# Decoder block: order of the first layer's scan decays on ScalarE, one half step moved ahead of the rotary block, one Newton step fewer

## The reference

```
x = x + attention0(layernorm(x))            # 8 heads, 2 kv heads, d = 32, rotary, window 64, softcap 30
x = x + ssm0(ctx, gate = layernorm(x))      # scan over ctx (4, 256, 128), 256 channels, 16 states
x = x + ffn0(layernorm(x))                  # 704 wide, SiLU gate
```

```
u     = silu(conv(in_proj(ctx)) + b)                    # 256 channels
dt, B, C = x_proj(u)                                    # 8 + 16 + 16 rows
delta = softplus(dt_proj(dt) + b)
state = state * exp(delta * A) + (delta * u) * B_t      # per channel and per state n of 16
y     = sum_n(state_n * C_n) + D * u ;  y *= silu(gate)
```

## Time and profile before

| | |
|---|---|
| median of 3 runs | 913.36 us (910.98 to 916.4) |
| the profiled execution's own time | 913.75 us |
| its span, first to last instruction | 912.0 us |
| mean granted TensorE clock | 0.924 |
| busy: PE / DVE / ACT / POOL | 767.7 / 703.3 / 445.6 / 340.6 us |
| chain that ended last | PE 50%, DVE 26%, issue 11%, ACT 9% |

### The profile page before, as it was taken

The page is one execution under the profiler, slowest core; times in us unless marked ns, Lnnn a source line. Parts: engine busy times, 40 slices in busy tenths (PEclk is TensorE's granted clock), DMA queues, the critical chain, the costliest instruction groups (busy, mean ns, idle before and its releaser), DMA issues.

```text
span 912.0 us, 12288 instructions
## 1 busy us (share of the span) xinstructions
PE 767.7 (84%) x3984; PEld 563.1 (62%) x3984; DVE 703.3 (77%) x1229; ACT 445.6 (49%) x928; POOL 340.6 (37%) x242
## 2 busy tenths in 40 slices
PE   6771459877798996799999999999955799999997
PEld 2241346554433563477767776777743689999996
DVE  4869779889857976999999999999977544444443
ACT  1663368650336402666566556756642354444442
POOL 1001346552330422233333323432343286666663
PEclk9785579998799998999999999999987899999999
DMA  4313223345020212011111211111300243334431
GB/s 171 121 47 114 93 94 125 115 139 218 1 98 0 74 43 92 19 40 44 51 36 36 69 36 36 55 39 36 118 0 1 79 158 138 138 138 138 141 135 46
DMA packets 28884, 74.63 MB, mean 82 GB/s; under 512 B 3633, under 2 KB 6337, under 8 KB 28449
## 3 DMA queue, kind: packets, MB, share of 16 engines
q1 hardware_dynamic: 28384, 71.51, 23.2%
q10 hardware_dynamic: 448, 2.49, 0.8%
HBM read 72.55 MB, written 1.44 MB: 81 GB/s over the span
## 4 chain that ended last, share of the span: by engine, by line
PE 50%; DVE 26%; issue 11%; ACT 9%; POOL 3%; DMA 1%; POOLq 0%; DVEq 0%; SPq 0%; ACTq 0%
PE ps L1671 6%; PE ps L1785 6%; PE ps L1786 6%; PE ps L1787 6%; PE ps L1631 4%; DVE hS L976 3%; PE ps L1651 3%; PE ps L1750 3%; PE ps L1435 2%; PE ps L1738 2%; DVE arena L1280 2%; DVE hS L1006 2%; DVE ps L968 2%; PE ps L1408 1%; PE ps L1720 1%
## 5 line engine op out<-in xcount | busy, mean ns | idle before, releaser
L403 POOL TENSOR_TENSOR hS<-hS,BCb 128x512 f32<-128x512 f32 x64 | 81.6, 1278 | 131.9 <-issue 66.7
L1387 DVE SCALAR_TENSOR_TENSOR arena<-ps,arena 128x1024 f32<-128x1024 f32 x32 | 39.2, 1224 | 102.2 <-ACT arena L842 93.1
L426 POOL TENSOR_TENSOR hS<-hS,BCb 128x1024 f32<-128x1024 f32 x23 | 56.1, 2440 | 111.3 <-DVE ps L968 96.3
L1671 PE MATMUL ps<-WB,hT 128*128 128x512 f32 x192 | 88.0, 603 | 3.0 <-DVE arena L1261 2.0
L476 POOL TENSOR_TENSOR MHl<-arena,MHh 128x1024 fp32r<-128x1024 f32 x34 | 81.7, 2404 | 16.9 <-ACT MHh L845 16.9
L1416 PE MATMUL ps<-ident,hS 128*128 128x128 f32 x256 | 40.1, 311 | 54.7 <-POOL hS L426 31.2
L1785 PE MATMUL ps<-Wh,MHh 128*128 128x256 f32 x272 | 77.8, 286 | 6.0 <-POOL MHl L476 6.0
L1006 DVE TENSOR_TENSOR_SCAN hS<-dA,ps 128x512 f32<-128x512 f32 x64 | 78.1, 1220 | 2.2
L1786 PE MATMUL ps<-Wl,MHh 128*128 128x256 f32 x272 | 77.6, 285 | 0.0
L1787 PE MATMUL ps<-Wh,MHl 128*128 128x256 f32 x272 | 77.5, 285 | 0.0
L1416 PEld LDWEIGHTS ps<-ident,hS 128*128 128x128 f32 x256 | 32.6, 159 | 65.1 <-POOL hS L426 38.2
(11 more groups left out here) (233 smaller groups left out, 1967.4 us busy)
## 6 DMA issues: line engine op xcount, KB each, us to landing
BCb<-bc_dram SPq DMA_DIRECT2D x32, 512.0 KB, 3.7
BCb<-bcq_dram SPq DMA_DIRECT2D x64, 256.0 KB, 3.1
arena<-gate_dram SPq DMA_DIRECT2D x32, 512.0 KB, 3.7
WB<-in_we SPq DMA_DIRECT2D x34, 256.0 KB, 2.7
WB<-in_wqkv SPq DMA_DIRECT2D x1, 3072.0 KB, 12.7
WA<-in_wo ACTq DMA_DIRECT2D x1, 2048.0 KB, 7.7
WA<-in_ffn SPq DMA_DIRECT2D x1, 1408.0 KB, 7.9
pkb<-in_pk SPq DMA_DIRECT2D x2, 698.0 KB, 4.7
```

Of the source, the lines that this page charges most:

```text
L403: gp.tensor_tensor(h, h, qbc(q)[:, 1:2, :].broadcast_to([P, DT, S]), ALU.mult).then_inc(s["c_ready"], 1)
L426: gp.tensor_tensor(h, h, BCb[g % SB_LOADS][:, 1:2, :].broadcast_to([P, DT, HALF]), ALU.mult).then_inc(s["c_ready"], 1)
L1671: last = mm(ps[:, bank + t, :], hT[:, c, P * (2 * b + t):P * (2 * b + t) + P], WB[:, c, c0:c0 + 512], start=(c == 0), stop=(c == HC - 1))
```

## The change

On ScalarE the decays of half steps 1, 2 and 3 are issued in a row, ahead of `xdbl_copy(1)`. Before, those of half step 1 stood between the copy and the softplus, those of 2 behind the softplus, those of 3 behind the eight projection copies. On VectorE half step 3 is run ahead of the rotary block and not behind it. The reciprocal square root has three Newton steps and not four.

```diff
             steps_to(0)
             d_u(0)
+            steps_to(3)
             xdbl_copy(1)
-            steps_to(1)
             softplus(1)
             softplus_ln(1)
-            steps_to(2)
             for t in range(NT):
                 act.wait_ge(s["qkv0_mm"], t + 1)
                 sc.copy(Q0[:, t, :], ps[:, 4 + t % 4, 0:NQKV0]).then_inc(s["qkv0_copied"], 1)
-            steps_to(3)
             d_u(1)
...
             delta_u(1)
+            ssm_step(3)
             dve.wait_ge(s["qkv0_copied"], NT)
...
-            for g in range(3, 6):
+            for g in range(4, 6):
                 ssm_step(g)
...
-            for k in range(4):
+            for k in range(3):
...
-                if k < 3:
+                if k < 2:
```

## The result

The change makes the kernel faster, by less than forecast: 911.38 us median (908.92 to 914.04) against 913.59 (910.98 to 923.67), 20 runs each; ratio 0.9968 with a 95% interval of 0.9955 to 0.9981. The ratio makes 2.9 us (1.7 to 4.1), where 4.89 were forecast; the two medians lie 2.2 us apart. The profiled execution took 910.91 us, its span is 909.1, the mean granted clock 0.923.

A forecast was written before the change was run, and what follows sets the result against it. Order of work bounds the early part, VectorE's own work the later. 4.01 us gained at half step 4's scan (8.46 idle removed, 4.36 added) and 0.88 from the Newton step make 4.89: median 908.5 us, range 904.5 to 914.

The forecast's parts named there:

- Decays ahead, VectorE up to the block: Before the rotary block: early decays fit ScalarE's idle time at no cost; VectorE is free for the block 3.64 us sooner.
- The eight copies: Projection copies ahead of the rotary block: TensorE goes on without a stop, the last ends at 57.7, before VectorE's 58.80.
- The added wait: Ahead of half step 4's scan: VectorE waits 4.36 us for decays queued behind the square of the heads and a table load.
- Newton step: In the reciprocal square root ahead of L1111: three dependent instructions go, and the whole 0.88 us is gained.
- L1111: VectorE's scaling of the heads, ahead of the first attention: starts at 92.66 instead of 97.55, 4.89 us earlier.
- To the end: From L1111 to the kernel's end: the 4.89 us lead arrives whole, as nothing there is tied to a point in time.
- rival of a cheaper start: At the attention's 32 transposes: TensorE's clock rises earlier against them; about 1.5 us more gives 907.0; chance 0.10, faster.
- The range and the sign: For the whole kernel: a gain, with the time between 904.5 and 914 us.
- the chance of faster by over 0.5%: For the whole kernel: faster 0.56, against within 0.5% 0.36 and slower 0.08.
- The rivals on the clock: Projection copies late, about 911, chance 0.10; transposes cheaper, 907.0, chance 0.10; FFN matmuls at half clock, slower, chance 0.08.

The follow-up runs named there:

- e8: The change run again unaltered, to see its clock: 910.13 us, one run.
- e3: The change with the decays of half steps 4 to 7 put ahead of the square of the heads: 905.62 us, ratio 0.9908 to before.
- e2: The change with four Newton steps, so the two moves alone: 910.86 us, ratio 0.9964 to before.
- e4: The change with 44 unread identity transposes in TensorE's quiet time between the C transposes of half steps 7 to 10: 911.53 us, ratio 0.9968 to before.
- e11: The change run again unaltered, to see its clock and waits: 911.24 us.
- e5: The change with half step 3 put back behind the rotary block on VectorE: 908.67 us, ratio 0.9949 to before.
- e6: The kernel before, run again unaltered to see its clock: 916.39 us, one run.
- e7: The kernel before, run again unaltered to see its clock: 915.88 us, one run.
- e9: The kernel before, run again unaltered to see its clock: 913.77 us.
- e10: The kernel before, run again unaltered to see its clock: 913.29 us.
- e1: The kernel before with three Newton steps and the old order: 912.8 us, ratio 0.9987 to before.

## Why the prediction was right, and where it was not

- **Decays ahead, VectorE up to the block.** Right. Scans 1 and 2 forecast at 40.95 and 45.68, found at 41.34 and 46.06, all shifted by the 0.40 us that the first B product started later; the block forecast 26.11 behind it, found 26.06.
- **The eight copies.** Right in effect: last one at 55.49, ahead of VectorE. Its detail was off: TensorE's clock rose at 46.4 in the change and not at 49, TensorE did stop, for 0.32 us, and the clock stayed at 1.0 to the end of the projection. The copies were early by luck of the clock, which was also up from 39.5 to 43.0. In e8, where it rose at 48.8, TensorE had no stop and the last copy ended at 57.73, where 57.7 was forecast.
- **The added wait.** Right: 4.40 for 4.36. e3 shows it by removing it.
- **Newton step.** 0.89 at L1111 (e2 against the change). At the end no experiment resolves it.
- **L1111.** Forecast 4.89 us ahead, found 4.94 behind the first B product. All terms of the sum held to 0.1 us.
- **"To the end" is the step that failed.** It said that what is ahead at L1111 arrives whole, since nothing later is tied to a point in time. In the pair of profiles 5.16 us at scan 8 became 2.9 at the second division, by TensorE's clock, and was 2.6 at 232 us and 2.9 at the end. In this pair the rise of the clock did not move with the work. e4 shows the cause at that place by removing it, and the waits of the 14 profiles go by the length of the stretch at half clock. The sum put this term at nothing. My rival of a cheaper start came true too, 0.6 us at scan 8, and was outweighed.
- **How much of it is systematic.** The mean of five profiles of before and three of the change gives L1111 4.5 us apart, the third division 4.2 and the end 4.3. So 0.4 is missing at L1111 because one before in five had the sooner preparation; behind it 0.5 is gained up to scan 8 and 0.8 lost in the waits. The waits for units 0 and 1 were 0.55 to 3.05 us in before and 1.3 to 2.8 in the change; they overlap. The ratio of the 20 runs gives 2.9 (1.7 to 4.1). Of the five profiles with the decays of 1 to 3 moved and those of 4 to 7 behind the square (the change, e8, e11, e2, e5) four have the long stretch at half clock, of the six in the old order (before, e6, e7, e9, e10, e1) one; that the change meets it more often is likely, not shown. Eight profiles can't settle the 1.4 us between 4.3 and 2.9, which stay open.
- **The range and the sign** held; the chance of faster by over 0.5% (0.56) was too high for 0.32%, because one profile's sum was carried through 800 us, and no rival put a loss by the clock at the attention's first units, where VectorE already waited 0.63 us for TensorE. The rivals on the clock stood at the projection, at the transposes and at the FFN. At the FFN the rise came at 250.4 us in before and at 247.8 in the change, 2.6 apart like the work, and nothing was lost.

## What to carry to other kernels

When work is moved out of the cover of a long instruction, look at what the cover was hiding: here the table load and the first decays behind a square. Put both ahead of the instruction that waits (e3) and the gain is 8.4 us instead of 2.9 (by the ratios). A lead of a few us ahead of a stage in which a fast engine waits for TensorE in short bursts should be given a loss term from the granted clock, taken from several profiles, before it is booked in full.

## What the runs showed of the hardware

- A rise of TensorE's granted clock from 0.5 to 1.0 need not follow a shift of the work. In the pair of profiles the work came 5 us earlier and the rise at 135.1 us instead of 134.3, while at the FFN it moved with the work. Over five executions of the same kernel before it came at 133.8 to 139.4 us.
- VectorE's waits in the attention's first units went by the length of the stretch at half clock: 0.55 to 0.65 us with 10.2 to 10.3 us of it, 2.57 to 3.05 with 17.0 to 17.1.
- Filling one quiet stretch with transposes kept the clock at 1.0 from 113.6 to 161.4 us, but the next stretch at half clock, 165.8 to 169.2 us in the change, became one of 161.4 to 171.7 and cost 2.3 us more. That is one profile with the filling; in the 13 without it this stretch lasted between nothing and 6.9 us.
- The kernel before, unchanged, spread over 911 to 917 us in most runs. Its first B product started at 32.18 to 33.53 us; its five profiles differ by up to 3.6 us in the end behind the first B product, 2.0 of which can arise in the second pair's preparation alone.
